# Weight transposes moved out of the feed-forward loop into the attention stage, and two more PSUM banks in the second Hadamard pass

## What is computed

```
x = x + layernorm(gated_delta(layernorm(x), Wq, Wk, Wv, Wo, Wb, bb, Wd, bd))
x = x + layernorm(ffn(layernorm(x), W1, W2, W3))

ffn(x):                                   # D = 2048, H = 8192
    hidden = silu(x @ W1.T) * (x @ W3.T)  # W1, W3: [H, D]
    hidden = fwht(hidden)                 # Walsh-Hadamard over the 8192, normalized
    return hidden @ W2.T                  # W2: [D, H]
```

## Time and profile before

| | us |
|---|---|
| three runs | 6939.14, 7158.01, 7214.44 (median 7158.01) |
| the profiled execution | 6928.74 |
| its span, first to last instruction of the slowest core | 6927.2 |
| spans of the 8 cores | 6908.9 to 6927.2, mean granted clock 0.739 to 0.741 on each |
| TensorE busy | 3860.4 (56%) |
| VectorE busy | 1305.3 (19%) |
| ScalarE busy | 936.3 (14%) |
| start of stage 3, 4, 5, 6 in the span | 1078, 1481, 4316, 5493 |

### The profile page before, as it was taken

One profiled execution on the slowest core, in us unless ns is written; L12 is line 12 of the kernel. 1 busy time (PEld: TensorE's weight loads), 2 busy tenths in 40 slices (PEclk: granted clock), 3 DMA queues, 4 the chain that ended last, 5 costly groups with the idle time before them and its releaser, 6 DMA issues.

```text
span 6927.2 us, 51520 instructions; the slowest of 8 cores (6908.9 to 6927.2 us)
## 1 busy us (share of the span) xinstructions
PE 3860.4 (56%) x16400; PEld 1650.5 (24%) x16400; DVE 1305.3 (19%) x3213; ACT 936.3 (14%) x2120; POOL 123.0 (2%) x172
## 2 busy tenths in 40 slices
PE   0132342238888888888888887111111387877840
PEld 0011110013333333333333333000000133333310
DVE  1023235531111221121112211111111100000013
ACT  1132323431111111111111111000000000000012
POOL 1000000000000000000000000000000000000000
PEclk9655555558888888888888888555555698999975
DMA  9911101221111111111111111961111236373445
GB/s 126 123 46 37 49 31 61 85 61 37 37 37 37 37 37 37 37 36 37 36 36 35 36 36 33 117 87 60 59 57 58 79 125 157 126 167 122 128 136 170
DMA packets 500718, 493.13 MB, mean 71 GB/s; under 512 B 306800, under 2 KB 446064, under 8 KB 487152
## 3 DMA queue, kind: packets, MB, share of 16 engines
q1 hardware_dynamic: 173248, 260.21, 11.1%
q0 software_dynamic: 143152, 103.76, 10.5%
q10 hardware_dynamic: 184064, 125.87, 9.7%
HBM read 441.58 MB, written 142.61 MB: 84 GB/s over the span
## 4 chain that ended last, share of the span: by engine, by line
PE 47%; DMA 27%; DVE 12%; issue 7%; ACT 6%; DVEq 1%; SPq 0%; ACTq 0%; POOL 0%; POOLq 0%
PE pA L679 15%; DMA g_b<-zbs 13%; PE pA L688 13%; DMA zfl_b<-zfs 7%; PE pT L315 6%; PE pM L815 5%; DMA xt_s<-xp 4%; PE pOT L815 2%; PE pP L815 2%; DVE stat_s L271 2%; DVE zfr_b L757 2%; ACT w1t_b L325 2%; DVE w1t_b L320 2%; PE pA L343 2%; DMA out<-x1t_s 1%
## 5 line engine op out<-in xcount | busy, mean ns | idle before, releaser
L679 PE MATMUL pA<-xn2T_b,w1t_b 128*128 128x512 bf16 x4096 | 1071.9, 421 | 37.7 <-DVE w3t_b L320 37.7
L688 PE MATMUL pA<-xn2T_b,w3t_b 128*128 128x512 bf16 x4096 | 925.8, 379 | 0.0
L815 PE MATMUL pM<-zfl_b,w2t_b 128*128 128x512 bf16 x2048 | 659.0, 391 | 222.9 <-DMA zfl_b<-zfs 220.5
L753 PE MATMUL pA<-g_b,hb_s 128*128 128x512 bf16 x256 | 139.6, 597 | 1038.1 <-DMA g_b<-zbs 1003.5
L315 PE MATMUL pT<-idn_s,xnb_s 128*128 128x128 bf16 x768 | 182.4, 264 | 953.1 <-ACT xnb_s L301 855.9
L679 PEld LDWEIGHTS pA<-xn2T_b,w1t_b 128*128 128x128 bf16 x4096 | 429.6, 106 | 629.2 <-issue 245.7
L688 PEld LDWEIGHTS pA<-xn2T_b,w3t_b 128*128 128x128 bf16 x4096 | 400.9, 98 | 483.2
L703 DVE TENSOR_TENSOR hid_b<-hid_b,pA 128x512 bf16<-128x512 bf16 x256 | 176.2, 688 | 1742.0 <-PE pA L688 1725.2
L315 PE MATMUL pT<-idn_s,w1n_b 128*128 128x128 bf16 x1024 | 254.0, 248 | 414.3 <-DVE w1t_b L320 235.7
L815 PE MATMUL pOT<-zfl_b,w2t_b 128*128 128x512 bf16 x1024 | 401.7, 392 | 0.0
L815 PE MATMUL pP<-zfl_b,w2t_b 128*128 128x512 bf16 x1024 | 400.7, 391 | 0.0
(11 more groups left out here) (111 smaller groups left out, 2354.8 us busy)
## 6 DMA issues: line engine op xcount, KB each, us to landing
zfl_b<-zfs SPq DMA_DIRECT2D x256, 512.0 KB, 3.7
w2s<-w POOLq DMA_DIRECT2D x32, 1024.0 KB, 182.4
xt_s<-xo ACTq DMA_DIRECT2D x32, 1024.0 KB, 4.8
w1n_b<-w POOLq DMA_DIRECT2D x64, 512.0 KB, 3.4
w3n_b<-w POOLq DMA_DIRECT2D x64, 512.0 KB, 25.2
zbs<-zbr_b SPq DMA_DIRECT2D x64, 512.0 KB, 8.3
g_b<-zbs SPq DMA_DIRECT2D x64, 512.0 KB
zfs<-zfr_b SPq DMA_DIRECT2D x64, 512.0 KB, 2.8
```

Of the source, the lines that this page charges most:

```text
L679: k.op("tensor", lambda t, dt=dt, ts=ts, par=par: t.matmul(pA0[:], w1t[:, par * D + dt * 128:par * D + (dt + 1) * 128], xn2T[:, dt * TH + ...
L688: k.op("tensor", lambda t, dt=dt, ts=ts, par=par: t.matmul(pA1[:], w3t[:, par * D + dt * 128:par * D + (dt + 1) * 128], xn2T[:, dt * TH + ...
L753: k.op("tensor", lambda t, o=gb.start + i * 512, b=bank: t.matmul(b[:], hb2[:], gbuf[:, o:o + 512], start=True, stop=True), inc=s_t)
L815: base=base: t.matmul(banksC[dt][:], w2t[:, base + a1 * 512 + dt * 128:base + a1 * 512 + (dt + 1) * 128], zfl[:, o:o + 512], start=(a1 == ...
```

## The change

The 64 chunks of W1 and W3 are transposed ahead of stage 4 and kept in DRAM (`w1ts`, `w3ts`, bf16). The new function `emit_wprep_block` handles the next chunk c: POOL waits (for c < 2 for the last projection, otherwise for both writes of chunk c - 2) and issues the two casting loads into a quarter of `xnT` each; TensorE does the same 32 transposes, emptied in place by VectorE and ScalarE; SP waits for both and issues the two writes of 512 KB. One call stands at the end of each of the 17 steps of the own segment's pair loop, three at the end of each of the 16 `tau` steps; together they cover the 64 chunks. In stage 4, POOL loads `w1t` and `w3t` ready-made from DRAM, and the 32 transposes are gone; the loads of c + 2 now wait for the last matmul of c. In stage 5 the four matmuls of a group go to four PSUM banks instead of two in turn; stage 6's first two banks take over the release of those that stage 5 used.

```
+    w1ts = nc.dram_tensor("w1ts", [NC, 128, D], BF16, kind="Internal").ap()
+    w3ts = nc.dram_tensor("w3ts", [NC, 128, D], BF16, kind="Internal").ap()
+    def emit_wprep_block():
+        c = wprep["next"]
+        if c >= NC:
+            return
+        wprep["next"] += 1
+        par = c % 2
+        b1 = xnT[:, par * D:(par + 1) * D]
+        b3 = xnT[:, 2 * D + par * D:2 * D + (par + 1) * D]
+        if c < 2:
+            k.wait("gpsimd", s_t, wprep["proj_done"])
+        else:
+            k.wait("gpsimd", s_wpw[par], wprep["written"][c - 2])
+        k.dma("gpsimd", b1, w1r_[c], s_wp[par])
+        k.dma("gpsimd", b3, w3r_[c], s_wp[par])
+        wl = s_wp[par].n
+        k.wait("tensor", s_wp[par], wl)
+        for dt in range(NDT):
+            emit_transpose(b1[:, dt * 128:(dt + 1) * 128], b1[:, dt * 128:(dt + 1) * 128],
+                           128, evac_eng=("vector" if dt % 2 == 0 else "scalar"))
+            emit_transpose(b3[:, dt * 128:(dt + 1) * 128], b3[:, dt * 128:(dt + 1) * 128],
+                           128, evac_eng=("scalar" if dt % 2 == 0 else "vector"))
+        k.wait("sync", s_v, s_v.n)
+        k.wait("sync", s_a, s_a.n)
+        k.dma("sync", w1ts[c], b1, s_wpw[par])
+        k.dma("sync", w3ts[c], b3, s_wpw[par])
+        wprep["written"][c] = s_wpw[par].n
...
         for p in range(NP + 1):
             if p < NP:
                 emit_pair_indep(p, is_own)
             if p > 0:
                 emit_pair_dep(p - 1, is_own)
+            if is_own:
+                emit_wprep_block()
...
         xnb_free[par] = (s_t, s_t.n)
+        emit_wprep_block()
+        emit_wprep_block()
+        emit_wprep_block()
...
+        if c == 0:
+            k.wait("gpsimd", s_wpw[0], s_wpw[0].n)
+            k.wait("gpsimd", s_wpw[1], s_wpw[1].n)
         if c >= 2:
             sem, val = wtrans_done[c - 2]
             k.wait("gpsimd", sem, val)
-        k.dma("gpsimd", w1n[:, dsl], w1r[c], s_wl[par])
-        k.dma("gpsimd", w3n[:, dsl], w3r[c], s_wl[par])
+        k.dma("gpsimd", w1t[:, dsl], w1ts[c], s_wl[par])
+        k.dma("gpsimd", w3t[:, dsl], w3ts[c], s_wl[par])
...
-        for dt in range(NDT):
-            emit_transpose(w1n[:, par * D + dt * 128:par * D + (dt + 1) * 128],
-                           w1t[:, par * D + dt * 128:par * D + (dt + 1) * 128], 128,
-                           evac_eng=("vector" if dt % 2 == 0 else "scalar"))
-            emit_transpose(w3n[:, par * D + dt * 128:par * D + (dt + 1) * 128],
-                           w3t[:, par * D + dt * 128:par * D + (dt + 1) * 128], 128,
-                           evac_eng=("scalar" if dt % 2 == 0 else "vector"))
-        wtrans_done.append((s_t, s_t.n))
...
+    banks4 = (pA0, pA1, pM0, pOT)
+    cbank = [(s_v, 0)] * 4
         for i in range(4):
-            bpar = i % 2
-            bank = pA0 if bpar == 0 else pA1
-            sem, val = cbank[bpar]
+            bank = banks4[i]
+            sem, val = cbank[i]
...
-    cmb_free = [(s_v, 0)] * 4
+    cmb_free = [cbank[2], cbank[3], (s_v, 0), (s_v, 0)]
```

More of the change, by code:

```diff
@@ L189, in build_nc @@
     s_wl = [k.sem("s_wl0"), k.sem("s_wl1")]
+    s_wp = [k.sem("s_wp0"), k.sem("s_wp1")]
+    s_wpw = [k.sem("s_wpw0"), k.sem("s_wpw1")]
     s_xt = [k.sem("s_xt0"), k.sem("s_xt1")]
@@ L327, in emit_transpose @@
         return tp_free[par]
+    w1r_ = w1_d.rearrange("(h1 j c) d -> c j h1 d", h1=64, j=2, c=64)
+    w3r_ = w3_d.rearrange("(h1 j c) d -> c j h1 d", h1=64, j=2, c=64)
+    wprep = {"written": {}, "next": 0, "proj_done": 0}
+    def emit_wprep_block():
[24 more added lines that the diff above has]
+        wprep["written"][c] = s_wpw[par].n
     proj_bank = {"free": [(s_v, 0), (s_v, 0)]}
@@ L529, in emit_segment @@
         k.wait("tensor", s_v, elt_done)
+        if is_own:
+            wprep["proj_done"] = s_t.n
         for p in range(NP + 1):
@@ L598, in build_nc @@
         xnb_free[par] = (s_t, s_t.n)
+        emit_wprep_block()
+        emit_wprep_block()
+        emit_wprep_block()
     x1_all_written = s_x1w.n
     xn2T_v, xn2T_a = s_v.n, s_a.n
+    while wprep["next"] < NC:
+        emit_wprep_block()
     k.barrier()
@@ L605, in build_nc @@
     bmark = al.mark()
-    w1n = al.sb("w1n_b", [128, 2 * D], BF16)
-    w3n = al.sb("w3n_b", [128, 2 * D], BF16)
     w1t = al.sb("w1t_b", [128, 2 * D], BF16)
@@ L611, in build_nc @@
     zbr = al.sb("zbr_b", [128, 2 * TH], BF16)
-    w1r = w1_d.rearrange("(h1 j c) d -> c j h1 d", h1=64, j=2, c=64)
-    w3r = w3_d.rearrange("(h1 j c) d -> c j h1 d", h1=64, j=2, c=64)
     wtrans_done = []
@@ L654, in build_nc @@
             k.wait("tensor", s_a, xn2T_a)
-        for dt in range(NDT):
-            emit_transpose(w1n[:, par * D + dt * 128:par * D + (dt + 1) * 128],
-                           w1t[:, par * D + dt * 128:par * D + (dt + 1) * 128], 128,
-                           evac_eng=("vector" if dt % 2 == 0 else "scalar"))
-            emit_transpose(w3n[:, par * D + dt * 128:par * D + (dt + 1) * 128],
-                           w3t[:, par * D + dt * 128:par * D + (dt + 1) * 128], 128,
-                           evac_eng=("scalar" if dt % 2 == 0 else "vector"))
-        wtrans_done.append((s_t, s_t.n))
-        wt_v, wt_a = s_v.n, s_a.n
         if c >= 2:
@@ L674, in build_nc @@
             k.wait("tensor", sem, val)
-            if ts == 0:
-                k.wait("tensor", s_v, wt_v)
-                k.wait("tensor", s_a, wt_a)
             for dt in range(NDT):
@@ L709, in build_nc @@
                 emit_bp(bst["pend_bp"].pop(0))
+        wtrans_done.append((s_t, s_t.n))
         zb_written.append(None)
@@ L732, in build_nc @@
     zfr_free = [(s_v, 0)] * 2
-    cbank = [(s_v, 0), (s_v, 0)]
+    banks4 = (pA0, pA1, pM0, pOT)
+    cbank = [(s_v, 0)] * 4
     k.wait("sync", s_zbw[0], s_zbw[0].n)
@@ L754, in build_nc @@
                 b[:], hb2[:], gbuf[:, o:o + 512], start=True, stop=True), inc=s_t)
-            cmm = s_t.n
-            k.wait("vector", s_t, cmm)
+            cmms = s_t.n
+            k.wait("vector", s_t, cmms)
             k.op("vector", lambda v, o=zb_.start + i * 512, b=bank: v.tensor_scalar(
                 zfr[:, o:o + 512], b[:], RS, None, OP.mult), inc=s_v)
-            cbank[bpar] = (s_v, s_v.n)
+            cbank[i] = (s_v, s_v.n)
         gfree[r] = (s_t, s_t.n)
```

## The result

The changed kernel is slower: 7242.29 us median of ten runs (7154.46 to 7574.83) against 7053.58 us for the kernel before (6932.47 to 7349.69). The ratio of undisturbed runs is 1.0313, 95% interval 1.0257 to 1.0369. Both kernels' runs spread by several per cent because in some executions the cores of a die are granted a lower clock; the ratios leave those out, and no trace of such an execution was kept. The range of the prediction, 7030 to 7490, holds the measured time; its figure of 7162, held against the 7158.01 that stood there as the time of before, says that nothing changes, and that did not come.

A forecast was written before the change was run, and what follows sets the result against it. Stage 4 was taken as bound by TensorE's own order, its loads hidden behind matmuls. Terms 345 + 898 - 29 - 966 - 15 = +233 us on a span of 6927.2 gave 7162 with 1.5 us outside it; range 7030 to 7490.

The forecast's parts named there:

- the pair loop: Loop before stage 3 that takes 17 of the new blocks; forecast +345 us (+280 to +382).
- Stage 4's gain: Stage 4 without its transposes: a chunk falls from 43.78 to 28.48 us, -966 us in all.
- Rival 2: In stage 4 TensorE's clock doesn't hold: 7482 at 0.85 of the clock, 7580 at 13/16; chance 0.20.
- The loop of transfers sets the pace: In the pair loop, writes, reload and transposes of a buffer, 39.5 us + W, outlast TensorE's 36.2 us of work.
- W: Time for a new block's two writes: 12 us in the pair loop (3.9 to 16.6), 4.4 in stage 3.
- Block 0: First new block, in the pair loop behind its first step; its loads were to land at 998.9.
- The first turn: Pair loop: one round of writes, reload and transposes, two blocks long; every turn was forecast at 51.5 us.
- Stage 3 with the entry: Stage 3's steps of 83.4 us, +898 us, together with a quicker entry into stage 4, -29 us.
- block c: Third block of a stage-3 step: it reuses the first's buffer, so waits for its writes and a 26.35 us load.
- the late `xt` load: In stage 3, the `xt` load meets block writes and loads on the same engines; 2 us added a step.
- Stage 5: Four PSUM banks close a 0.24 us gap of VectorE in each of 64 groups: -15 us.
- Two engines for a load: Each casting load of W1 and W3 uses two of 16 DMA engines, hence about 25 us to land.

## Why the prediction was right in its parts and wrong in its number

- **What failed is the last step of the sum.** I made it on the profiled execution (6928.7) and gave 7162 as the time of the kernel, while the time of before as shown was a median of 7158.01. Read against that, 7162 says no change at all, although the text gives 0.84 to slower by over 2%. Against its own kind, the profiled execution of the changed kernel (7183.54), the sum was 22 us short: 6.5 in the pair loop, 6.9 in stage 3 and the entry, 1 in stage 4, 4 in stage 5 and 3.3 in the rest. The sum stood for a ratio, 7162 / 6928.7 = 1.034, and the measured ratio is 1.0313 (1.0257 to 1.0369). Carried over to the median it would have been 7158 x 1.034 = 7400; over ten runs the median of before turned out to be 7053.58, which gives 7291, and 7242.29 was measured. I named the difference between the two bases and then used only the one that the trace came from. The three runs shown were no good base either: their median lay 1.5% above that of ten.
- **Stage 4's gain** was right: 964.8 us measured, 966 forecast. Rival 2, the clock, did not come in the execution of which there is a trace: 1.00 over 1740 us in which TensorE is busy all the time, a chunk every 28.5 us. The Trainium skill's box on the peak-current limiter ("TensorE: Matmul & The Clock Gate") speaks against that row; by its 13/16 a chunk would take 35.1 us, an estimate, and the trace does not agree.
- **The loop of transfers sets the pace**: right, and shown from both sides, by the faster load and by more buffers.
- **W**, the term I trusted least, was 12 in the pair loop against 13.2 in the mean, and 4.4 in stage 3 against 4.5, both with the hand-over to POOL in the measured figure. The pair loop came out right partly by luck. Block 0 began at 1002.97, 4 us later than counted, as the last projection ended later. The first turn took 44.0 us instead of 51.5, as its writes met no load, which I had not seen. The other seven took 53.0 each, 10.5 us more in all. Together +7, so +351.5 stands against +345. (The recorded line "1311 + 100" should read 999 + 412; its total, 1411, is right.)
- **Stage 3 with the entry**: 875.9 against 898 - 29 = 869. The step came out right with two small errors that cancel. In the step from 1512.87 to 1597.49 the tau step took 27.5 us (25.2 and 2 for `xt` forecast), the blocks 12.1, 11.7 and 11.9 (12.4 each), the wait for block c 19.8 (19.1), and there was a wait of 1.6 for block b, which I had taken as loaded. Over the 15 steps that wait is 1.2 in the mean. The guess of 2 us for the late `xt` load held.
- **Stage 5**: 11.1 against 15, the one term too large by a quarter.
- **Rival 2's figures**, 7482 and 7580, were worked out on the span, not on the time of the kernel: each is about 2 us low.
- **Two engines for a load**: read from 0.26 and 0.54 of the DMA engines, and shown by the split, by the count of packets and by the share of 1.04 in stage 5. The Trainium skill ("DMA: Bandwidth & Descriptors", on why a DMA increments its semaphore by 16) also has the rule that fits: the number of engines is the largest up to 16 that divides the slowest dimension of both patterns. I weighed the same page's fit of bytes over bandwidth (it stands there under "Anatomy of one DMA — SWDGE (gpsimd) path", not where the prediction puts it), and not this rule, which names both the fault and its remedy. The traces agree with it at 25 and 6.2 us in one place, 14 and 5.6 in the other.

## What to carry to other kernels

Work that is moved out of a stage where matmuls cover its loads must be priced where it lands: there its load, its write and the wait for the buffer count in full unless as many buffers turn as the latency needs. Before moving work, make it cheap where it stands: 32 small transposes with a copy each took 13.3 us a chunk, packed eight to a bank 4.4, and nothing had to move. And a forecast made on one profiled execution is a ratio; say it as one, and carry it over to the base that the time will be held against.

## What the runs showed of the hardware that I had not expected

- VectorE empties 1024 bf16 columns from PSUM in 0.68 us and 128 in 0.225; ScalarE in 1.01 and 0.266. Eight times the columns cost three to four times the time.
- How the transposes are issued decides what the matmuls behind them cost: behind 4.4 us of packed transposes 16 matmuls took 3.61 us (the level of 2.4 GHz), behind 13.3 us of single ones 6.00 us.
- 512 KB stores that land in 2.6 us alone take 8.3 beside two casting loads; in the changed kernel's stage 4, where no such load is in flight, the same `zbs` writes land in 2.6 us, median. They also do in the kernel before with its casting loads split in two.
